# Recurrent step on one core: the column for the next pick goes through both layers ahead of the four first-layer products

## The reference, cut to what matters

```
def step(h, p):
    op = jnp.argmax(h[0, 0, :NOPS])
    ...
    h = jnp.where(p['am'][op], y, h)
    z = jax.nn.relu(h @ p['w1'][op] + p['b1'][op]) @ p['w2'][op] + p['b2'][op]
    h = jnp.where(p['fm'][op], z, h)
    return (h, None)
```

## Time and profile before

| | |
|---|---|
| median of 3 runs | 128.83 us (128.76 to 129.32) |
| span of the profiled execution | 127.3 us |
| PE busy | 114.2 us, 90% of the span |
| DVE busy | 74.4 us, 58% |
| ACT busy | 68.3 us, 54% |
| chain that ended last | PE 59%, DVE 21%, ACT 12%, issue 6% |

### The profile page before, as it was taken

How to read it: one execution, slowest core, us unless ns; L and a number is a source line. 1 busy time by engine, 2 the same in 40 slices (tenths; PEclk the granted TensorE clock), 3 DMA queues, 4 the chain that set the end, 5 groups by cost and what they waited for, 6 DMA issues and landing times.

```text
span 127.3 us, 3032 instructions
## 1 busy us (share of the span) xinstructions
PE 114.2 (90%) x1200; PEld 82.3 (65%) x1201; DVE 74.4 (58%) x149; ACT 68.3 (54%) x121; POOL 25.9 (20%) x34
## 2 busy tenths in 40 slices
PE   6989889998989899997977899999999987989990
PEld 5667566577423325877966678888888975656750
DVE  0076976718984362129999599699493004346241
ACT  4254796357630407027978959969956631347000
POOL 8996000004940000002616050050000000000000
PEclk9999999999999999999999999999999999999997
DMA  3544000000101000000000000000000000000002
GB/s 106 168 56 110 12 0 5 0 1 8 34 0 31 3 17 14 5 5 0 0 0 5 0 0 5 0 0 5 0 8 0 0 8 0 0 0 0 5 0 88
DMA packets 3060, 2.22 MB, mean 17 GB/s; under 512 B 1570, under 2 KB 2754, under 8 KB 3040
## 3 DMA queue, kind: packets, MB, share of 16 engines
q0 software_dynamic: 464, 0.67, 2.7%
q1 hardware_dynamic: 2144, 0.74, 2.4%
q10 hardware_dynamic: 432, 0.55, 1.2%
HBM read 1.68 MB, written 0.26 MB: 15 GB/s over the span
## 4 chain that ended last, share of the span: by engine, by line
PE 59%; DVE 21%; ACT 12%; issue 6%; DVEq 0%; ACTq 0%
PE ps L977 9%; PE ps L489 5%; DVE smat L913 5%; PE ps L991 5%; PE ps L1001 4%; PE ps L1293 4%; PE ps L514 3%; PE ps L496 3%; PE ps L276 3%; PE ps L287 3%; ACT tx L848 2%; DVE smatT L740 2%; PE ps L518 2%; PE ps L655 2%; ACT rstd L530 2%
## 5 line engine op out<-in xcount | busy, mean ns | idle before, releaser
L913 DVE TENSOR_TENSOR smat<-ty,tx 128x1536 f32<-128x1536 f32 (+1 forms) x14 | 21.5, 1555 | 4.3 <-ACT tx L848 4.2
L954 ACT ACTIVATE smatT<-ps 128x1536 f32<-128x1536 f32 x12 | 17.4, 1450 | 7.8 <-PE ps L977 7.6
L977 PE MATMUL ps<-cst,smat 128*128 128x128 f32 x144 | 18.1, 275 | 2.6 <-DVE smat L913 2.3
L977 PEld LDWEIGHTS ps<-cst,smat 128*128 128x128 f32 x144 | 15.7, 140 | 4.3 <-DVE smat L913 3.2
L489 PE MATMUL ps<-cst 128*128 128x256 f32 x48 | 13.0, 387 | 0.3 <-issue 0.3
L1001 PE MATMUL ps<-samp,wc 128*128 128x128 f32 x72 | 11.0, 291 | 0.0
L991 PE MATMUL ps<-smatT,xt 128*32 128x96 f32 x384 | 10.4, 249 | 0.4 <-ACT samp L945 0.4
L1001 PEld LDWEIGHTS ps<-samp,wc 128*128 128x128 f32 x72 | 8.9, 191 | 1.6
L489 PEld LDWEIGHTS ps<-cst 128*128 128x128 f32 x48 | 8.3, 190 | 2.2 <-issue 1.3
L830 POOL TENSOR_SCALAR disty<-disty 128x288 f32<-128x288 f32 x3 | 6.2, 2081 | 17.2 <-ACT disty L837 17.2
L991 PEld LDWEIGHTS ps<-smatT,xt 128*32 128x32 f32 x384 | 7.9, 109 | 2.3 <-issue 1.8
(11 more groups left out here) (200 smaller groups left out, 198.1 us busy)
## 6 DMA issues: line engine op xcount, KB each, us to landing
cst<-in_cst ACTq DMA_DIRECT2D x1, 278.0 KB, 3.5
x<-in_x SPq DMA_DIRECT2D x2, 128.0 KB, 2.9
ew<-in_L_ffn_weight POOLq DMA_DIRECT2D x4, 64.0 KB, 2.2
ew<-in_L_ffn_weight POOLq DMA_DIRECT2D x1, 256.0 KB, 4.2
w<-in_L_ffn_ffn_w SPq DMA_DIRECT2D x3, 64.0 KB
cst<-in_cst ACTq DMA_DIRECT2D x1, 129.0 KB, 3.0
out<-fin SPq DMA_DIRECT2D x1, 128.0 KB, 2.2
out<-fin ACTq DMA_DIRECT2D x1, 128.0 KB, 2.1
```

The costliest lines, as they stand in the source:

```text
L913: return nc.vector.tensor_tensor(smat[:, n % 3, BP * part.start:BP * part.stop, :].rearrange("p u (g r c) -> p (u g) r c", g=DG, c=W), ty[ ...
L954: nc.scalar.activation(smatT[:, n % 2, :, :, :].rearrange("p k g n -> p (k g n)"), ps[:, bank:bank + 3, :].rearrange("p b n -> p (b n)"), ...
L977: last = nc.tensor.transpose(ps[:, bank + u // BP, (u % BP) * P:(u % BP + 1) * P], smat[:, n % 3, u, :], ident)
```

## The change

On PE the two small matmuls that take the column through the second layer are moved ahead of the four large first-layer products. So is the wait for the column's relu (`l_rc`), and with it the waits for `w2` and `b2`; the wait for `b2` now stands between the two small matmuls. On DVE the pick is moved ahead of the relu of group 1. ACT, POOL and SP keep their order.

```
                 nc.tensor.matmul(ps[:, 6, 0:1], w1[0:C, p, :], u[0:C, 0:1], start=True, stop=True).then_inc(sem("l_hc"), 1)
+                pe.wait_ge(sem("l_w2_%d" % p), 16)
+                pe.wait_ge(sem("l_rc"), 1)
+                nc.tensor.matmul(ps[0:1, 5, 0:C], rcol[:, :], w2, start=True, stop=False)
+                pe.wait_ge(sem("l_b2_%d" % p), 16)
+                nc.tensor.matmul(ps[0:1, 5, 0:C], b2[0:C, p:p + 1], ident[0:C, 0:C],
+                                 start=False, stop=True).then_inc(sem("l_col"), 1)
                 for g in range(BP):
                     rows = slice(C * g, C * g + C)
                     nc.tensor.matmul(ps[:, g, :], w1[rows, p, :], u[rows, :],
                                      start=True, stop=True).then_inc(sem("l_hid"), 1)
-                pe.wait_ge(sem("l_w2_%d" % p), 16)
-                pe.wait_ge(sem("l_b2_%d" % p), 16)
-                pe.wait_ge(sem("l_rc"), 1)
-                nc.tensor.matmul(ps[0:1, 5, 0:C], rcol[:, :], w2, start=True, stop=False)
-                nc.tensor.matmul(ps[0:1, 5, 0:C], b2[0:C, p:p + 1], ident[0:C, 0:C],
-                                 start=False, stop=True).then_inc(sem("l_col"), 1)
...
+                self.pick(dve)
                 hidden(1)
-                self.pick(dve)
                 hidden(3)
```

## The result

The changed kernel took 129.81 us (median of 18 runs, 128.71 to 130.37). The kernel before, run beside it, took 129.07 (18 runs, 128.39 to 130.57), a little more than the 128.83 of its first three runs. The ratio is 1.005, with a 95% interval of 1.0029 to 1.0071: **0.65 us slower** (0.37 to 0.92) where 0.39 was forecast, which lies just inside that interval. The 129.81 lies above the range's 129.7, for two reasons: the base came out 0.24 higher than the three runs on which the forecast stood, and some executions paid a cost that I had put among the unlikely ones.

The account below looks back on a forecast made before the run. Each step was bound by large products, then DVE's relu, pick, relu and the last product; +0.37 us in step 0 and +0.02 in step 1 gave +0.39, 129.2 us, range 128.8 to 129.7.

Parts of the forecast that it names:

- a cost that I had put among the unlikely ones: Rival: PE idles longer within a step, its clock halves, 4.3 us more for both steps, 133 us; chance 0.03.
- The large products wait, the relus stand together: PE's first large load 1.4 us behind L652's in step 0, 1.1 in step 1; DVE's two relus 0.66 us apart.
- `b2` ends the wait in step 0: PE's second small matmul waits for b2's DMA, 2.92 us after issue, and loads at 35.57.
- the rival of a late `b2`: b2 lands later in step 0, delaying the products queued on PE: 0.33 us more, sum 0.72, 129.55 us; chance 0.09.
- The turn to the large products: On PE, from second small matmul to first large load, a changed tiling form drains the array: 0.15 us per step.
- the rival that puts it at 0.02: No drain on PE before the large products: 0.13 us less per step, sum 0.13, 128.95 us; chance 0.10.
- The four products together: PE's four large products, starting together, take 1.12 us; the rival said 1.33, sum 0.81, 129.65 us, chance 0.08.
- The early landing of `w1`: Between the steps, w1 comes 0.57 us earlier but gains nothing; rival: up to 0.33 us back, 128.9 us, chance 0.14.
- The pick is covered: In step 0 DVE finishes the pick at about 36.7, 0.3 us before its relu can start.
- the sign that I had named for SP: SP issues w1 near 37.7, yet L652 of step 1 still comes near 41.9.
- The clock: Rival: longer idle time on PE halves its clock, 4.3 us more for both steps, 133 us; chance 0.03.
- a sign of being wrong: The forecast would be wrong if the profile's clock row dips between 34 and 50 us.

Follow-up runs that it names:

- the second profile: The changed kernel, unchanged, run and profiled again beside the kernel before: ratio 1.001 (0.9977 to 1.0042).
- the first profile: The changed kernel's first run against the kernel before: 129.81 us, ratio 1.005.
- both gaps filled: Changed kernel plus one matmul without a reader behind L652 and one behind the four large products, in each step: 1.0002 of the kernel before.
- the second profile of before: The kernel before, unchanged, profiled again; clock 1.00, three stretches of the two steps sum to 11.10 us as at first.
- the two later runs: The changed kernel, unchanged, run twice more against the kernel before: ratios 1.001 and 1.0022.
- The three filled kernels: Changed kernel plus a matmul without a reader behind L652, behind the four large products, or at both places: 0.9999, 0.9999 and 1.0002 of the kernel before.
- PE's part alone: Kernel before with only PE's order changed, DVE keeping relu, pick, relu: ratio 1.0167 (1.0122 to 1.0213).
- the kernel without L496: Kernel before without its matmul without a reader behind the second layer (0.86 us of columns per step): ratio 0.998 (0.9947 to 1.0012).

## Why the prediction was wrong

- **The large products wait, the relus stand together: right.** The load came 1.50 us behind L652's in step 0 of the second profile (34.34 to 35.84; forecast 1.47) and 1.17 in step 1 (42.95 to 44.12 in the first profile; forecast 1.12). Relus 1.41 as forecast.
- **`b2` ends the wait in step 0: right,** 0.39 us of idle time with that load as its end. It shows only where the step starts on time. In the four profiles where it decides, filled ones included, `b2` was used 2.93 to 3.10 us behind its issue (forecast 2.92), short of the 0.25 more from which the rival of a late `b2` would decide.
- **The turn to the large products: right in size,** 0.14 us from L657's loads to L661's (35.85 to 35.99) where 0.15 was taken, so the rival that puts it at 0.02 falls. That the 0.14 are a drain, no run shows.
- **The four products together: right.** From their load to ACT's relu, which follows by 0.03, 35.99 to 37.15: 1.13 against 1.12, not 1.33.
- **The early landing of `w1`: right that it gives nothing back.** With both gaps filled `w1` was issued 3.81 us ahead of step 1's first load (37.97 to 41.78) instead of 3.25, and the same 0.33 us of idle time stands in front of that load, now put down to "issue", as it is in the second profile of before.
- **The pick is covered: wrong in step 0.** I had DVE free 0.3 us before the relu can start. In all six profiles with the changed order, filled or not, that relu starts 0.42 to 0.43 us behind the pick's last instruction, as the relu behind the pick did before; in step 1 the distance is 0.57, and the products decide. The pick's first instruction took 0.32 to 0.59 us instead of 0.16 (last section). Going by step 1, where DVE's relu starts 0.04 us behind ACT's, step 0's is 0.03 to 0.31 late. Where step 0 started on time, it took 4.21 to 4.30 us, not 4.16. In the sum this was made up for by terms that I had too high: those 0.04, where the forecast has 0.13 (0.16 less 0.03), and the time between the steps, 3.42 to 3.48 instead of 3.52 at full clock. For the same reason the sign that I had named for SP didn't come: in the unfilled kernel it issued `w1` at 38.21 to 38.25, not near 37.7.
- **The clock: the step that failed.** I gave a fall 3 in 100 and priced it at 4.3 us, as if it lasted through both steps. It came in 15 of 42 executions, and the dip between 34 and 50 us that I had named as a sign of being wrong is in the first profile. The three profiles that have it show it in one step, twice step 0 and once step 1. By medians those executions were 0.8, 0.8 and 1.15 us longer than the rest of their run; only one, with a mean clock of 0.955, took 132.93 us, near the 133 of my price. A third of 0.8 to 1.15 is some 0.3 to 0.4 us. With the 0.4 of the traces this makes 0.7, against 0.65 measured at first, but 0.13 and 0.29 in the two later runs. My argument was that the clock also stays at 1.00 where PE works 5.99 of 8 us. That is 75%; ahead of the fall it was 57%, so that row was no bound for this place.

What stays open: the forecast's 0.39 is seen in traces, in no whole time. The three filled kernels are at 1.000 with intervals of 0.35%, and the changed kernel's executions at full clock lie 0.47 above, 0.35 below and level with the kernel before that ran beside them. A reason is that what lies behind the two steps scatters by more: from the end of step 1's last relu to the end of the span it took 81.3 to 82.4 us in the profiles of the two kernels and the filled ones, all but the one with its fall in step 1. So the split of the measured time between the steps' own terms and the clock is argued from traces and from executions with and without a fall, not shown. Nor is it settled why idle time behind the second layer left the clock alone.

## What to carry to other kernels

Moving a small dependent chain ahead of large independent work in an in-order queue exchanges one wait for another: count the waits that the large work inherits (here a DMA that had been covered), look whether the engine that takes the small piece earlier is free by then (here an older copy was still open), and look whether another engine can take the late piece instead, which here gave 1.1 to 1.4%. When a change makes TensorE idle between bursts, look at the granted clock of many executions, not at one profile: a fall in a third of them is a mean cost that one trace shows whole or not at all. One filling matmul in either gap was enough to keep it.

## What the runs showed of the hardware

The clock fell to half although PE never stood still in the loop for longer than 0.76 us (the idle time ahead of L665, in all three traces that show a fall). The same 0.76 us stand at 1.00 in the profile of PE's part alone, and 1.36 us in one piece in the kernel without L496. The Trainium skill (TensorE: Matmul & The Clock Gate, What's actually happening) has the gate follow how busy PE has been; the fillings agree with that, the kernel without L496 does not by its busy share alone.

In step 0 a copy of 16 x 128 on DVE (L1442) is open for 5.0 us in every trace. The pick's first instruction, started at 35.59 to 36.18 in the six profiles with the changed order, ended within 0.01 us of the copy's end in all of them (36.50 in the two above); in step 1 the same instruction took 0.17. A relu that started with the copy still open, 35.76 before, took its usual 0.75, but it too ended behind the copy (36.51 against 36.45). POOL fills memory at that time, and the copy ends 0.06 to 0.09 us behind the last of its fillings in all 14 traces; before, that is

```profile
35.82 0.56 POOL L1185 MEMSET xtw<- 128x256 f32 x2
```

The Trainium skill (SBUF — State Buffer, SBUF: two separate sides) says that some DVE instructions and GpSimd need the same pair of ports, which one of them holds for its whole instruction while the other waits. The copy's end behind POOL's would fit that. No run here changes POOL's work or the copy, so none tells whether that is the cause.
